# Attention with its heads side by side on four row groups of TensorE

## The reference

```
h = layernorm(x) * (1 + ca) + sa
q = rope(h @ wq);  lat = h @ w_down;  k = rope(lat @ wk_up);  v = lat @ wv_up
scores = (q . k) / sqrt(8), masked so that a query sees the pages of 32 keys up to its own
x = x + ga * (softmax(scores) @ v) @ wo
h = layernorm(x) * (1 + cb) + sb
four times: cur = cur + sum over the top 2 of 4 experts of w_e * (gelu(cur @ W1_e + b1_e) @ W2_e + b2_e)
x = x + gb * cur
```

## Time and profile before

| | us |
|---|---|
| median of 3 runs | 771.0 (769.58 to 771.03) |
| profiled execution, its own time | 771.94 |
| its span, first to last instruction | 770.1 |
| PE, DVE, ACT, POOL busy | 681.2, 588.5, 520.4, 183.8 |
| preparation and its transfers, to the first bin | 0 to 75.45 |
| bins ahead of the first score | 75.45 to 107.06 |
| attention | to 340.96 |
| projection and second norm | to about 368 |
| experts | to the end |

### The profile page before, as it was taken

One profiled execution on the slowest core, in us unless ns is written; L12 is line 12 of the kernel. 1 busy time (PEld: TensorE's weight loads), 2 busy tenths in 40 slices (PEclk: granted clock), 3 DMA queues, 4 the chain that ended last, 5 costly groups with the idle time before them and its releaser, 6 DMA issues.

```text
span 770.1 us, 12222 instructions
## 1 busy us (share of the span) xinstructions
PE 681.2 (88%) x3976; PEld 427.2 (55%) x4000; DVE 588.5 (76%) x1133; ACT 520.4 (68%) x905; POOL 183.8 (24%) x144
## 2 busy tenths in 40 slices
PE   3920988999699999987599999999999999999996
PEld 2410222333233333345478777787777877778885
DVE  5670987888588888229678898888988889888775
ACT  2530035677476777973488888888888888888984
POOL 0451016000000000000223343333433344322322
PEclk9965579999899999998799999999999999999998
DMA  9541041100101000000111110011100111101200
GB/s 237 150 139 65 0 117 40 43 21 25 46 2 44 24 20 4 3 1 1 66 45 55 56 56 28 29 56 56 55 34 24 54 56 57 54 2 55 69 15 28
DMA packets 17413, 37.20 MB, mean 48 GB/s; under 512 B 3305, under 2 KB 11241, under 8 KB 14533
## 3 DMA queue, kind: packets, MB, share of 16 engines
q1 hardware_dynamic: 16037, 34.65, 13.9%
q10 hardware_dynamic: 1312, 1.74, 0.9%
HBM read 31.86 MB, written 4.33 MB: 47 GB/s over the span
## 4 chain that ended last, share of the span: by engine, by line
PE 33%; DVE 12%; issue 5%; ACT 1%; POOL 0%; POOLq 0%; DVEq 0%
DVE gel_lo L1049 6%; PE y L952 6%; PE y L954 5%; PE y L953 5%; PE hid L943 5%; PE hid L942 5%; PE hid L941 5%; PE plog L963 2%; DVE part L1105 1%; ACT gel_hi L1017 1%; DVE at_least L1077 1%; PE pcw L972 1%; DVE cw L1096 0%; DVE cw L1094 0%; DVE dl L1084 0%
## 5 line engine op out<-in xcount | busy, mean ns | idle before, releaser
L1049 DVE TENSOR_TENSOR gel_lo<-gel,gel_hi 128x512 fp32r<-128x512 f32 x256 | 248.3, 1010 | 6.7 <-ACT gel_hi L1017 5.7
L588 DVE TENSOR_REDUCE mcol<-mx 128x1 f32<-128x512 f32 (+2 forms) x320 | 193.1, 635 | 61.7 <-PE mx L704 58.8
L562 ACT ACTIVATE probs<-st 128x512 f32<-128x512 f32 x288 | 155.7, 596 | 99.3 <-PE st L660 57.1
L1016 ACT ACTIVATE gel<-hid,b_sb 128x512 f32<-128x512 f32 x256 | 176.1, 688 | 38.5 <-PE hid L943 16.2
L1017 ACT ACTIVATE gel_hi<-hid,b_sb 128x512 fp32r<-128x512 f32 x256 | 174.7, 682 | 0.0
L1157 POOL TENSOR_TENSOR cur<-cur,part 128x512 f32<-128x512 f32 x64 | 106.4, 1663 | 250.8 <-DVE part L1105 250.8
L704 PE MATMUL mx<-ks,qs 125*128 125x512 bf16 (+3 forms) x384 | 120.8, 364 | 38.3 <-PEq L208 32.0
L952 PE MATMUL y<-gel_hi,w_hi 128*128 128x512 f32 x256 | 104.4, 408 | 0.4 <-DVE gel_lo L1049 0.2
L941 PE MATMUL hid<-cur_hi,w_hi 128*128 128x512 f32 x256 | 102.2, 399 | 0.4 <-DVE cur_lo L1123 0.4
L943 PE MATMUL hid<-cur_hi,w_lo 128*128 128x512 f32 x256 | 102.2, 399 | 0.0
L942 PE MATMUL hid<-cur_lo,w_hi 128*128 128x512 f32 x256 | 102.1, 399 | 0.0
(11 more groups left out here) (147 smaller groups left out, 521.9 us busy)
## 6 DMA issues: line engine op xcount, KB each, us to landing
cwb<-gate_rows SPq DMA_DIRECT2D x16, 1024.0 KB, 4.7
ks<-in_k_rows SPq DMA_DIRECT2D x3, 640.0 KB
qs<-in_q_rows SPq DMA_DIRECT2D x3, 616.0 KB
q_pieces<-pieces_q SPq DMA_DIRECT2D x4, 384.0 KB, 4.8
k_pieces<-pieces_k SPq DMA_DIRECT2D x4, 384.0 KB, 6.0
ks<-k_pieces SPq DMA_DIRECT2D x8, 192.0 KB
qs<-q_pieces SPq DMA_DIRECT2D x8, 192.0 KB
x_sb<-in_x SPq DMA_DIRECT2D x4, 256.0 KB, 5.2
```

What stands on the lines that cost most here:

```text
L562: nc.scalar.activation(probs[u % SLOTS][:, h, :], st[:, (HG * u + h) % ST_RING, :], ACT.Exp, scale=SCALE).then_inc(exp_done, 1)
L588: nc.vector.tensor_reduce(mcol[a % SLOTS][:, h, slot:slot + step * (len(blocks) - 1) + 1:step], mx[:, at % MX_RING, 0:len(blocks) * keys]. ...
L1016: nc.scalar.activation(gel[n % RING][:, :], hid[n % RING][:, :], ACT.Gelu_apprx_tanh, bias=bias)
L1049: nc.vector.tensor_tensor(gel_lo[n % RING][:, :], gel[n % RING][:, :], gel_hi[n % RING][:, :], ALU.subtract).then_inc(lo_ok, 1)
```

## The change

The q and k of a head are split into two pieces of the type float32r instead of three of bfloat16, which makes three products: 24 rows, two rows for the maximum and four for the page mask, 30 of 32. So four heads lie below each other in one slot of 128 partitions, each on one row group of the array (`HROWS` = 32).

- Preparation: one piece less for ScalarE and GpSimd; rows are stored once for each of the three products, to DRAM in the order of the slot, constants too; a group's load is one transfer a side. At the end of TensorE's part 19 matmuls of 512 columns are added whose results nobody reads (`BUSY_PREP`).
- A unit has queries of one chunk only, so ten units make a group, two of 256 columns. A block on the diagonal is a matmul of its own (with the mask rows), 128 columns wide.
- A bin holds two heads in two banks (`PAIRS`), filled by pairs of matmuls on two row groups and reduced by one instruction. Ahead of it go matmuls on the full array without use (`keep_busy`): five in the first four bins, two or three up to the first score, then one a unit.
- In a step all four scores of unit k come first, with the two bins between them, and then the values of unit k − 1 in one piece, in one bank.
- The split of the maxima moves to GpSimd, in two pieces; four small transfers instead of one carry them.
- The loops are written out.

The core of the diff:

```diff
-Q_PIECE = [0, 0, 0, 1, 1, 2]
-K_PIECE = [0, 1, 2, 0, 1, 0]
+Q_PIECE = [0, 0, 1]
+K_PIECE = [0, 1, 0]
+HROWS = 32
+BUSY_PREP, BUSY_RISE, BUSY_FIRST, BUSY_LATER = 19, 5, 2, 1
...
 def load_group(sp, m, g, s):
-    for first, n in LOADS:
-        rows = slice(first * D, (first + n) * D)
-        sp.dma_start(m.ks[s][rows, :, :],
-                     m.kp[0:n, g].rearrange("c (d h) t -> c d (h t)", d=D)).then_inc(m.qk_in[s], 16)
...
+    for dst, src in ((m.ks[s], m.kp), (m.qs[s], m.qp)):
+        sp.dma_start(dst[:, :].bitcast(F32), src[g].rearrange("h r t -> (h r) t")).then_inc(m.qk_in[s], 16)
...
+            pe.wait_ge(h_ok, NCH)
+            for i in range(BUSY_PREP):
+                nc.tensor.matmul(turned[i % 2][:, :], m.ident[:, :], m.x[:, 0:TPC, :], start=True, stop=True)
...
-    ST_RING, MX_RING = 3, 3
+    ST_RING, PROBS, MX_RING = 3, 3, 2
...
+                for j, off, q0, nq in blocks:
+                    own = P if j // TPC == c else 0
+                    for rows, x, w in ((ROW_END, 0, own), (ROW_PAGE, own, nq - own)):
+                        if w:
+                            mm = nc.tensor.matmul(st[:, n % ST_RING, off + x:off + x + w],
+                                                  m.ks[s][r0:r0 + rows, j * P:(j + 1) * P],
+                                                  m.qs[s][r0:r0 + rows, c * CH + q0 + x:c * CH + q0 + x + w],
+                                                  start=True, stop=True)
...
+                keep_busy(g, n)
...
+                        for i in range(PAIRS):
+                            r0 = HROWS * (2 * pair + i)
+                            if w:
+                                mm = nc.tensor.matmul(mx[:, at % MX_RING, i, x * keys + y:x * keys + y + w],
+                                                      m.qs[s][r0:r0 + rows, t * P:(t + 1) * P],
+                                                      m.ks[s][r0:r0 + rows, k0 + y:k0 + y + w], start=True, stop=True)
...
+            def keep_busy(g, n):
+                at = bin_at(g, n)
+                first = PAIRS * (NU + LEAD)
+                count = BUSY_RISE if at < 2 * PAIRS else BUSY_FIRST + g if NBINS * g + n < first else BUSY_LATER * (n % PAIRS == 0)
+                for i in range(count):
+                    nc.tensor.matmul(mx[:, at % MX_RING, i % 2, :], m.ks[g % SLOTS][:, 0:P], m.ks[g % SLOTS][:, 0:CH],
+                                     start=True, stop=True)
...
+            for k in range(STEPS):
+                scores(k, 0)
+                scores(k, 1)
+                bins(k + NU + LEAD, 0)
+                scores(k, 2)
+                bins(k + NU + LEAD, 1)
+                scores(k, 3)
+                if k >= 1:
+                    weigh(k - 1)
+            weigh(STEPS - 1)
```

More of the change, by code:

```diff
@@ L72 @@
 ]
[L73 to L75 removed]
+PAIRS = HG // 2
+NBINS = len(BINS) * PAIRS
 LEAD = 4
[L77 to L80, removed]
+TURN_AFTER = 2 * PAIRS
+BUSY_PREP, BUSY_RISE, BUSY_FIRST, BUSY_LATER = 19, 5, 2, 1
 class Mem:
@@ L443, in attention, with uses, bin_at, turn_at @@
         l.sem(n) for n in ("vs_init", "vs_ok", "w_in", "w_hi", "w_lo", "small_in"))
[L445 to L488, removed]
+    CHAIN = 3
+    STEPS = GROUPS * NU
+    def uses(g):
+        return g // SLOTS + 1
+    def bin_at(g, n):
+        return n if g == 0 else NBINS + (NBINS + 1) * (g - 1) + n + (n >= TURN_AFTER)
+    def turn_at(g):
+        return NBINS + (NBINS + 1) * g + (TURN_AFTER if g + 1 < GROUPS else 0)
+    def turn_due(m_unit):
+        g, u = divmod(m_unit, NU)
+        return g - 1 if 1 <= g <= GROUPS and u == TURN_AFTER // PAIRS - 1 else None
     with nc.Block() as block:
@@ L516, in _ @@
             sp.dma_start(m.tri[:, :, :, :], m.w["tri"]).then_inc(small_in, 16)
-            all_groups(sp, body)
+            load_group(sp, m, 2, 2)
+            for g in range(GROUPS):
+                max_rows(g)
+                if g >= 1 and g + 2 < GROUPS:
+                    sp.wait_ge(st_done, HG * NU * g)
+                    load_group(sp, m, g + 2, (g + 2) % SLOTS)
             sp.wait_ge(small_in, 112)
@@ L651, in _, with scores @@
+            for g in range(GROUPS):
+                for n in range(NBINS):
+                    if n == 1 and g >= 1:
+                        merge(g - 1)
+                    if n == TURN_AFTER and g >= 1:
+                        keep_rows(g - 1)
+                    read_bin(g, n)
+            merge(GROUPS - 1)
+            keep_rows(GROUPS - 1)
         @block.tensor
         def _(pe):
-            def scores(i, a, u, h):
-                s, n = a % SLOTS, HG * (NU * gnum(i, a) + u) + h
+            def scores(k, h):
+                g, u = divmod(k, NU)
+                s, n, r0 = g % SLOTS, HG * k + h, HROWS * h
+                c, blocks = UNITS[u]
@@ L724, in body @@
-            def body(i, a):
-                for u in range(NU):
-                    nxt, side = following(i, a, u), part_at(i, a, u)
-                    for half in range(2):
-                        if exists(*nxt[:2]):
-                            scores(*nxt, 2 * half)
-                            scores(*nxt, 2 * half + 1)
-                        if exists(*side[:2]):
-                            part(*side, 2 * half)
-                        weigh(i, a, u, half)
-                        if exists(*side[:2]):
-                            part(*side, 2 * half + 1)
-                    if side[2] == 0 and exists(i, a + 1) and not exists(*side[:2]):
-                        turn_maxima(i, a + 1)
@@ L740, in _ @@
-            nc.tensor.sem_inc(st_done, ST_CREDIT)
-            nc.tensor.sem_inc(exp_done, EXP_CREDIT)
-            nc.tensor.sem_inc(pv_done, PV_CREDIT)
-            nc.tensor.sem_inc(ov_read, OV_CREDIT)
-            for a, parts in ((0, NU), (1, LEAD)):
-                for p in range(parts):
-                    for quarter in range(4):
-                        part(0, a, p, quarter)
-            for h in range(HG):
-                scores(0, 0, 0, h)
-            all_groups(pe, body)
+                    own = P if k0 + keys == (t + 1) * P else 0
@@ new lines, in bins @@
+            def bins(unit, pair):
+                g, u = divmod(unit, NU)
+                if g < GROUPS:
+                    fill_bin(g, PAIRS * u + pair)
+                if pair == PAIRS - 1 and turn_due(unit) is not None:
+                    turn_maxima(turn_due(unit))
+            for unit in range(NU + LEAD):
+                for pair in range(PAIRS):
+                    bins(unit, pair)
+            for k in range(STEPS):
+                scores(k, 0)
[6 more added lines that the diff above has]
+                    weigh(k - 1)
```

393 lines of the change are left out of this document (159 added, 234 removed).

## The result

| | median us | lowest to highest | ratio to before [95%] |
|---|---|---|---|
| before | 770.29 | 769.29 to 771.03 | |
| after | 887.32 | 878.09 to 908.16 | 1.146 [1.135, 1.157] |
| forecast | 745 (715 to 860) | | |

The changed kernel is 15% slower, and the prediction was wrong in sign and range. The executions of the changed kernel lie far apart, and the profiled one is the longest, 908.16 us with a span of 906.3. The others have a higher mean clock: 0.798 in the shortest, 0.761 in the profiled one. By spans of 876.2 and 906.3 us that is some 354 and 433 us at half clock (an estimate from these two means), so in the shortest the clock must have fallen later or come back for a while; which of the two is open, as only the longest was traced.

A forecast was written before the change was run, and what follows sets the result against it. It took PE to bound attention and transfers the preparation. First score at 99.5 + 185 for 66 steps + 29.4 tail + 1.5 ends attention at 315, for 340.96; 771.94 − 25.8 = 746.1, less 0.9: 745 us, range 715 to 860.

The forecast's parts named there:

- Preparation, first bin at 64: Before attention: transfers and 19 added matmuls end at 63 us, first bin at 64, 11 us earlier than before.
- First bins, 35.5 us: Bins before the first score: 28 pair-bins at mean 1.14 us plus 12 more bridges, 35 us; first score at 99.5.
- Row groups overlap: Attention's scores and bins: matmuls on two row groups run together, leaving four slots of 0.33 us, 1.32 a step.
- rival A: Attention: row groups do not overlap, eight slots, 4.1 us a step, 831 us in all; chance 0.27.
- A step at 2.80: Attention steps with bins: values, bridge, mode changes and four slots take 2.80 us (2.48 to 3.12), 66 times, 185 us.
- The tail, 14 × 2.1 + 1.5 = 31: Attention's last 14 steps without bins: 2.1 us each, 29.4, plus 1.5 for the last values; attention ends at 315.
- The rest: Outside preparation and attention, including the feed-forward part: nothing else moves.
- rival C: The clock falls to half: + 2.5 us for 66 steps, + 27 at the start, + 21 in the tail, 958; chance 0.16.

The follow-up runs named there:

- e4: The changed kernel without any full-array matmuls without use (bridges) in attention, those of the preparation kept: 844.59 us, 1.095 of the kernel before.
- e11: The changed kernel with four or five bridges ahead of each bin up to the first score, then one a step as changed: 892.0 us, 1.159 of before.
- e8: The changed kernel with two bridges ahead of every bin (four a step), three or four up to the first score: two executions, 899.82 and 936.58 us.
- e2: The kernel before with its score and bin matmuls cut to the first 32 of their rows, same order and type: 929.83 us, ratio 1.205.
- e9: The changed kernel with all 128 rows in score and bin matmuls and no bridges in attention: 777.02 us, 1.008 of the kernel before.
- e10: The kernel before with attention's outer loops written out and loads of groups 1 and 2 moved to the start of attention: 748.72 us, ratio 0.971.
- e1: The changed kernel with all 128 rows in every score and bin matmul instead of one row group, bridges kept: 794.25 us, 1.030 of the kernel before.
- e5: The kernel before with the outer loops of attention written out on every engine: 765.29 us, ratio 0.993.
- e6: The kernel before with each group's load in twelve transfers of 8 rows instead of transfers with outermost counts 3, 2 and 1: 772.75 us, ratio 1.003.
- e7: The kernel before with both the outer loops of attention written out and each group's load in twelve smaller transfers: 763.03 us, ratio 0.990.

## Why the prediction was wrong

By its own steps, on the profiled execution; 162 us lie between its 908.2 and the 746.1 worked out. It is the longest one: between the medians lie 142 us, and how these divide no trace shows. An execution in which the clock falls later has a smaller term for the first bins and the first steps.

- **Preparation, first bin at 64: nearly right.** It came at 60.47, 15.0 us earlier than before. As forecast, the 19 matmuls set it: 16.57 us from 43.60 (16.3 forecast), and no issue on SP is over 2.5 us. 3.5 us for the better.
- **First bins, 35.5 us: wrong by the clock.** (The terms give 34.6; the forecast went from 64 to 99.5.) 115.30 − 60.47 = 54.8 us, + 19.3. A bin was priced at 1.14 us and one with two bridges took 1.04 while the clock held; after the fall it took 1.76, and more with the third bridge. Without bridges (e4) the stage took 89.43 − 59.37 = 30.1 us even at half clock, near VectorE's own 29 as worked out. So the bridges, meant to carry the clock into the steps, cost 25 us here and did not carry it.
- **Row groups overlap: right, rival A is refuted.** Starts 0.01 us apart. Part 3 of "TensorE: Matmul & The Clock Gate" in the Trainium skill says row tiles start within nanoseconds of each other; the trace agrees as far as its 10 ns steps tell.
- **A step at 2.80: the failed step.** Its terms hold at full clock (2.95 to 2.98 by e11 and e8; bridge 0.225 for 0.227; two changes and a bridge 0.43 for 0.47). The step assumed the clock, and that was false: 4.64 us, 66 × 1.84 = + 121 us.
- **The tail, 14 × 2.1 + 1.5 = 31: wrong by the clock.** 475.6 − 115.3 − 66 × 4.64 = 54, + 23. ScalarE no longer sets it; PE at half clock does.
- **The rest: right.** −3.5 + 19.3 + 121 + 23 = 160, and the feed-forward part is as before.

So it is **rival C**, which had a chance of 0.16 and stood outside the range. Two arguments against it failed. "From 321 to 340 us the clock held" spoke of matmuls on all 128 rows, and no row of before had PE at work on 32; it was evidence on the wrong object. "Values and bridge are 1.1 us of each step at full array" took a share of full depth as enough; e11 shows that it is not. What the trace did show, half the clock over full-depth bins for 30 us, should have weighed more: it showed that a busy PE can stand at half clock in this kernel, and the change only made its matmuls shallower. C was also priced too high, 5.3 us a step and 958 in all: half the clock does not double a step. A bridge with its changes goes from 0.43 us (e11, 113.30 to 113.73) to 0.72 (255.30 − 254.58), values of 512 columns from 1.00 (112.93 − 111.93) to 1.86 (253.74 − 251.88). One bridge more costs 0.225 us at full clock and 0.42 at half (three take 1.58 us, two 1.16, in the change's first bins), so the streams nearly double, and what stands around them does not.

On the rule weighed in the prediction: Part 1 of "TensorE: Matmul & The Clock Gate" in the Trainium skill says that sustained matmul activity releases the throttle. e2 stands at 0.50 with PE busy 50.00 of 50 us. That and e4 at 0.50 with PE busy 93.95 of 100 us, beside e9 at 1.00 with the same instructions at full depth, show that the engine's busy share alone does not decide it here.

**Would it have paid at full clock?** With 2.95 or 2.98 in place of 2.80, the forecast's 745 becomes 755 to 757, or 751 to 753 with the preparation as it was, beside 749 for e10. And ten such steps are 29.5 to 29.8 us a group, for 29.27 before: the packed matmuls would have gained nothing a group even then, and the gain would have been all from the preparation and the loops. e10 gets it from the order of the loads and the loops alone: its end of attention at 316.0 beside the forecast's 315.

## What to carry to other kernels

Before packing shallow matmuls beside each other, ask what the array's fill does to the clock: overlap was real here and worth 0.5 us a step (3.47 in e1 less 2.98), the clock cost 1.7 (4.64 less the same). A one-line test (cut the contraction of the existing matmuls to the new depth, as in e2, leaving all else) tells the clock's answer before anything is rewritten. And take a change apart before building it: here its parts beside the matmuls were worth more than the matmuls, and an edit that was not among them, the place of two groups' loads on a queue, paid as much as the forecast promised.

## What the runs showed of the hardware beyond what was expected

- In the steps the rows filled decide the granted clock at equal type and order, with PE busy 94 to 100% of the time: e2 against before 0.50 for 1.00, e4 against e9 the same. In the bins ahead of them full depth alone does not: 0.50 before, 0.59 in e9.
- The same pattern can hold 1.00 for over 200 us and then fall for good (e8, at some 287 us). Why then and not earlier no run here tells, and it was not tried further.
- Half the clock made a step 1.64 times (e8: 64.10 / 39.03) and 1.57 times as long (the change against e11: 12.46 / 7.93), not twice.
- Moving the loads of one more group out of the preparation brought the first bin 11.9 us forward (73.83 in e5 to 61.97 in e10), where cutting every load into smaller ones gave 4.7 (e6) and 1.6 (e7 against e5); a turn of the written loop cost 6.9 us (e5).
